# Order of the products of a quad: all bfloat16 products together, the float32 products with the edge weights behind them

## The reference

```
parts = [x[src], x[dst]] (+ [e of the layer before], from the second layer on)
e     = relu(concat(parts) @ We + be)
agg   = segment_sum(e * norm[:, None], dst)
x     = relu(concat([x, agg]) @ Wn + bn)
```

## Time and profile before

| | |
|---|---|
| Median of three runs | 2226.51 us |
| The three runs | 2226.42, 2226.51, 2234.25 us |
| Span of the profiled execution | 2225.8 us |
| Mean granted TensorE clock | 0.926 of 2.4 GHz |
| PE, DVE, POOL busy, share of the span | 87%, 65%, 47% |

### The profile page before, as it was taken

The page is one execution under the profiler, slowest core; times in us unless marked ns, Lnnn a source line. Parts: engine busy times, 40 slices in busy tenths (PEclk is TensorE's granted clock), DMA queues, the critical chain, the costliest instruction groups (busy, mean ns, idle before and its releaser), DMA issues. The chain is left out here.

```text
span 2225.8 us, 48362 instructions
## 1 busy us (share of the span) xinstructions
PE 1936.7 (87%) x14264; PEld 1459.2 (66%) x14264; DVE 1438.0 (65%) x4661; ACT 648.2 (29%) x1271; POOL 1042.2 (47%) x1015
## 2 busy tenths in 40 slices
PE   6777769999999997488888885999999969999995
PEld 3322225444454544378888865999999859999993
DVE  6999962223231412678898864777777658787885
ACT  0156871212121211233333332333333322111111
POOL 0588850000000000177777734666666347777770
PEclk8687879999999998699999997999999989999998
DMA  3023682000000000645555534777777445555551
GB/s 98 12 60 86 105 103 3 1 0 0 0 0 0 0 0 27 226 147 148 154 154 155 148 101 127 217 218 215 216 214 216 139 115 155 144 155 148 154 148 41
DMA packets 193650, 242.15 MB, mean 109 GB/s; under 512 B 56276, under 2 KB 120047, under 8 KB 192799
## 3 DMA queue, kind: packets, MB, share of 16 engines
q1 hardware_dynamic: 161023, 172.73, 27.7%
q0 software_dynamic: 31840, 57.21, 11.3%
q10 hardware_dynamic: 576, 9.44, 1.1%
HBM read 149.75 MB, written 69.88 MB: 99 GB/s over the span
## 5 line engine op out<-in xcount | busy, mean ns | idle before, releaser
L1514 POOL DMA_INDIRECT rows<-p_dram,src_i x864 | 827.4, 958 | 349.3 <-issue 239.3
L1746 DVE TENSOR_TENSOR agg_t<-psum,agg_t 128x128 f32 x1380 | 390.7, 283 | 192.1 <-PE psum L1625 170.6
L1605 PE MATMUL psum<-w_c,before 128*128 128x128 f32 x1840 | 411.1, 305 | 0.0
L893 PE MATMUL psum<-adj,parts 128*128 (+2 forms) x1750 | 339.8, 351 | 5.3 <-ACT agg L972 4.4
L1594 PE MATMUL psum<-p_sb,pair_src 128*128 x1032 | 230.4, 307 | 108.5 <-DVE pair_dst L1720 66.9
L1679 ACT ACTIVATE rows<-rows 128x512 f32<-128x512 f32 x216 | 136.1, 630 | 575.8 <-DVE rows L1739 575.8
L1730 DVE TENSOR_SCALAR hot_w<-col_f,dst_loc,weight 128x128 f32<-128x128 f32 x864 | 301.2, 353 | 0.5
L1605 PEld LDWEIGHTS psum<-w_c,before 128*128 128x128 f32 x1840 | 283.2, 194 | 0.0
L1266 POOL MEMSET agg_t<- 128x3200 f32 x1 | 2.8, 2764 | 589.9 <-POOLq L1029 589.9
L893 PEld LDWEIGHTS psum<-adj,parts 128*128 128x128 f16 x1750 | 153.0, 98 | 190.9 <-issue 23.6
L1601 PE MATMUL psum<-q_parts,hot_all 128*128 x2592 | 252.2, 220 | 0.0
(11 more groups left out here) (241 smaller groups left out, 2486.1 us busy)
## 6 DMA issues: line engine op xcount, KB each, us to landing
e_dram<-after SPq DMA_DIRECT2D x230, 256.0 KB
before<-e_dram SPq DMA_DIRECT2D x230, 256.0 KB
adj<-stage SPq DMA_DIRECT2D x196, 97.8 KB
pair_rows<-sorted_rows SPq DMA_DIRECT2D x129, 128.0 KB
rows<-p_dram,src_i POOLq DMA_INDIRECT x864
hot_all<-dst_rows ACTq DMA_DIRECT2D x2, 3072.0 KB, 14.7
p_dram<-p_sb SPq DMA_DIRECT2D x6, 384.0 KB
records<-record_of,place_i POOLq DMA_INDIRECT x128
```

Source lines behind the costliest of these rows:

```text
L893: mm = nc.tensor.matmul(psum[:, AGG_BANK, 0:n_cols], parts[:, w, part, :], adj[:, w, cols], start=(w == 0 and part == 0), stop=(w == WINDO ...
L1514: nc.gpsimd.indirect_dma_start(out=rows[:, b % ROWS, m * D:(m + 1) * D], out_offset=None, in_=p_dram, in_offset=bass.IndirectOffsetOnAxis( ...
L1605: mm = nc.tensor.matmul(o, before[:, q % BEFORE, m * P:(m + 1) * P], w_c[:], start=False, stop=True)
L1746: nc.vector.tensor_tensor(a, psum[:, A_BANKS[q % len(A_BANKS)], m * P:(m + 1) * P], a, ALU.add).then_inc(agg_on, 1)
```

## The change

In `products`, a quad's work is issued by kind in place of by tile: first (sorted quads) the four float32 products of line 1594, then the twelve bfloat16 products, then (second and third pass) the four float32 products with `w_c`. The number of instructions of each kind, their operands, the waits ahead of them and the release behind the last one stay. `start=True` now stands on the first product of the quad alone, and `skip_group_check=True` is new on these products. In a rest quad of the first pass, which has bfloat16 products alone, the order stays.

```diff
--- before.py
+++ after.py
@@ -1588,22 +1588,28 @@
                     pe.wait_ge(hot_t_on, b + 1)
                 if e_before is not None:
                     pe.wait_ge(before_in[q % BEFORE], 16 * (q // BEFORE + 1))
+                def sums(m):
+                    return psum[:, E_BANKS[q % len(E_BANKS)], m * D:(m + 1) * D]
+
+                if i is not None:
+                    for m in range(QUAD):
+                        nc.tensor.matmul(sums(m), pair_src[:, i % PAIRS, m, :],
+                                         t["p_sb"][:, bass.ds(values[m], 1), :],
+                                         start=(m == 0), stop=False, skip_group_check=True)
                 for m in range(QUAD):
-                    o = psum[:, E_BANKS[q % len(E_BANKS)], m * D:(m + 1) * D]
                     if i is not None:
-                        nc.tensor.matmul(o, pair_src[:, i % PAIRS, m, :], t["p_sb"][:, bass.ds(values[m], 1), :],
-                                         start=True, stop=False)
                         hot, window = pair_dst[:, i % PAIRS, m, :], values[QUAD + m]
                     else:
                         s = (b * QUAD + m) * P
                         hot, window = hot_all[:, s:s + P], values[(b % 2 + 2) * QUAD + m]
                     for part in range(3):
-                        mm = nc.tensor.matmul(o, hot, t["q_parts"][:, bass.ds(window, 1), part, :],
-                                              start=(part == 0 and i is None),
-                                              stop=(part == 2 and e_before is None))
-                    if e_before is not None:
-                        mm = nc.tensor.matmul(o, before[:, q % BEFORE, m * P:(m + 1) * P], w_c[:],
-                                              start=False, stop=True)
+                        mm = nc.tensor.matmul(sums(m), hot, t["q_parts"][:, bass.ds(window, 1), part, :],
+                                              start=(i is None and m == 0 and part == 0),
+                                              stop=(part == 2 and e_before is None), skip_group_check=True)
+                if e_before is not None:
+                    for m in range(QUAD):
+                        mm = nc.tensor.matmul(sums(m), before[:, q % BEFORE, m * P:(m + 1) * P], w_c[:],
+                                              start=False, stop=True, skip_group_check=True)
                 mm.then_inc(spread, 1)
 
             def turn_and_sum(q):
```

## The result

| | before | after |
|---|---|---|
| Median, us (range, runs) | 2228.99 (2226.42 to 2238.82, 5) | 2213.54 (2211.35 to 2220.12, 5) |
| Span of the profiled execution, us | 2225.8 | 2210.0 |

After / before is 0.9925, with a 95% interval of 0.9906 to 0.9945: the change saves 15.5 us between the medians and 15.8 us between the two profiled spans. Forecast were 2210.0 us and 16.5 us.

What follows compares the result with a forecast made beforehand. PE's own stream was taken to bound the second pass, POOL's gathers the first and third. 15.7 + 0.2 + 0.6 = 16.5 us off the 2225.8 span gives 2209.3, with 0.7 for the median 2210.0 us; range 2203 to 2221.

Steps and rivals of the forecast that it cites:

- The sum: All three passes: 0.2 us saved in the first, 15.7 in the second and 0.6 in the third, together 16.5 us.
- The price of a change of kind: PE's weight loads: each bfloat16 run pays 0.0555 us once, so a quad with three runs fewer saves 0.167 us.
- rival (c): PE's stream: the change of kind isn't what costs 0.0555 us, or the chip sees the order otherwise; 2226 us, chance 0.08.
- The queue behind sorted quads: Second pass: list load of 1.27 us delays addresses, sorted quads 0.11 us late, so 34 of them save only 0.06 each.
- Rival (a): Second pass: list load stays at 1.44 us, 34 sorted quads lose 3.7 us; 2215.7, up to 2218 us, chance 0.17.
- rival (b): Sorted quads don't starve and the third pass's POOL waits shrink with PE's work; 2204 to 2207 us, chance 0.15.
- The Trainium skill's 64 instructions for TensorE's queue: PE's queue: not counted on; with it every sorted quad would keep its 0.167 us, the sum 3.7 us lower.
- The run of twelve in rest quads: Rest quads: first address leads by 1.7 us where 0.9 would do, so all 0.167 us are kept.
- Rival (d): Rest quads: the run of twelve is paced by its addresses, 0.43 us more each; 2256 us with sorted ones, chance 0.06.
- the 81 ns per matmul at 128 columns: PE's load and matmul pairs: by this pace a rest quad takes 1.89 us, the time about 2239 us; chance 0.02.
- The start of the second pass: First four quads, partly at a granted clock of 0.50: change of kind at twice its price, 0.8 us saved.
- The third pass: 0.8 us at the start and 0.5 at the end, less lower-clock work: 0.6 off, ends 3 gained and 3 lost.

Runs made afterwards that it cites:

- e5: Changed kernel with each quad issued in two halves of two tiles, each ordered by kind, giving two runs of six bfloat16 products; 2220.16 us.
- e3: Kernel before, in its old order, with only the flags changed: the start flag on a quad's first product alone; 2227.59 us.
- e2: Kernel before with the new order in sorted quads alone, rest quads in the old order; 2231.31 us.
- e6: Changed kernel with a sorted quad's list load issued earlier, between the transposes and sums ahead of it, in the first and second pass; 2212.86 us.
- e10: Kernel before with fourteen float32 products of constants ahead of sorted quads that follow a sorted quad, in the first and third pass; 2228.97 us.
- e4: Changed kernel with the new order kept in the second pass alone, first and third pass as in the kernel before; 2212.64 us.
- e1: Kernel before with the new order in rest quads alone, sorted quads in the old order; 2219.71 us.
- e7: Changed kernel with SP's store in the second pass issued one quad later, behind the load of `before`; 2212.07 us.
- e8: Changed kernel with fourteen float32 products of constants ahead of sorted quads that follow a sorted quad, in the first and third pass; 2206.35 us.

## Why the prediction was right, step by step

**The sum.** Between the spans 15.8 us went: 0.6 in the first pass, 17.9 in the second (14.8 of them from the fifth quad on) and -2.8 in the third, with 0.1 outside. Forecast were 0.2, 15.7 (14.9 from the fifth quad on) and 0.6. The total is closer than its parts: the start of the second pass gave 2.3 us more than forecast and the third pass 3.4 less, and that the two nearly cancel is luck. The median is 3.5 us above the forecast: 0.7 in the span, 1.4 in an offset (I put a run's time 0.7 us above its span, but in every run with both numbers it lies 1.9 to 2.3 above; the profiled run of the kernel after took 2212.09 us for 2210.0), and 1.4 by which that run lies below the median.

**The price of a change of kind** was 0.0555 us a run, by two run lengths of two stages. e5 and the change measure 0.0535, and 0.160 per rest quad in place of 0.167: 11.2 us for 11.7. That it is the order which costs it, e3 shows; rival (c) is out.

**The queue behind sorted quads** was the unknown, and its account held: a list load of 1.27 us was taken, 1.24 measured, started 1.88 us ahead by forecast and 1.87 by the trace, with the store moved to its start. The sorted quads gave 3.1 us for the 3.2 forecast, which is in part luck too, since they did not give it where I put it: the 27 ordinary ones 27 x 0.121 = 3.3, the seven further ones 0.8, and the seven behind these lost 1.0, since there the store goes out 0.8 us ahead of a list load of 1.4 to 1.75 us. Rival (a) is what e2 has, rival (b) what e6 has in the second pass. 11.2 + 3.1 leave 0.5 of the 14.8 us; 0.3 of it is the difference between the rest quads' median and their mean (3.114 us before, 2.947 after). The Trainium skill's 64 instructions for TensorE's queue ("TensorE: Matmul & The Clock Gate", specification table) don't show here: with room for them no sorted quad could be late by the prediction's account, and the list load again starts with 17 loads and their matmuls to go. By the trace 16 loads have yet to start at each of the 41 list loads of the second pass from its sixth quad on, before and after alike, while the time to the quad goes from 1.77 to 1.87 us.

**The run of twelve in rest quads** wasn't paced by its addresses: 0.73 us in 1504.41 to 1505.14. Rival (d) is out. So is, for this kernel, the 81 ns per matmul at 128 columns of the same page's section "Back-to-back issue gap": it is 60 ns here.

**The start of the second pass**, 0.8 forecast, measured 3.1 (29.1 to 26.0 us for the first four quads). This size isn't settled. The three kernels with the old order in that pass (before, e3, e10) have 27.6 to 29.1 us there, the six with the new one 26.0 to 27.8: the means are 1.6 apart, and the ranges overlap. The pair compared here shows more than most would.

**The third pass** is the step that failed, in its sign: "mostly POOL covers that, not at the end. I take 0.6 off". It lost 2.8 us, just inside its ends. The sum had 0.8 us for the pass's start and 0.5 for its last quads, so it left 0.7 for work at the lower clock. The 0.8 did not come through: POOL's run is 378.6 us before and after. What lies behind POOL's last gather goes from 6.8 to 9.6 us. The last sorted quad, which I had named as the uncovered place, accounts for it: at the lower clock it is 4.24 - 2.77 = 1.47 us longer, and it starts 2.77 us ahead of the end of POOL's last gather (2158.0) in place of 4.27 (2176.52), 1.5 later. The work behind it gives 0.2 back.

This end is no accident of one trace. PE idles 0.5 to 0.8 us ahead of the last sorted quad in the three kernels with the old order and no added products there (before, e3, e4), and 3.4 to 4.2 us in the six with a new order, whole or in part (after, e1, e2, e5, e6, e7). From slot 111 on the first three take 15.2 to 15.5 us, the six 19.7 to 21.1. That the low clock is the cause of the longer quad, e8 shows.

So I had the mechanism and priced it too low. Part of the price was to be had: PE gets ready earlier by what it saves, the gather does not come earlier, so the idle time grows just where nothing lies on top. The rest was not: PE idles 3.55 us longer there, and 1.8 of it is the gather: behind its end on POOL, DVE's addition starts after 3.56 us, in place of 1.75. Why it lands so late (DVE waits 3.51 us for it, 0.45 before) is not settled; no run here tells it apart.

## What to carry to other kernels

Where PE is the bound, count the changes of kind in its stream, since each run of bfloat16 loads between float32 ones pays once more (0.0535 us here); then check that whatever feeds the long run (addresses, list loads) can lead it by the time that the old alternation gave it for free. A saving on an engine that waits elsewhere is not neutral: it turns into idle time, and the next work can start at a lower clock (six of seven such quads of the third pass after, three before), which costs where nothing covers it. Filling such gaps with products of constants paid where they were longer than the filling (e8), and not where most of them were shorter (e10).

## What the runs showed of the hardware

A list load of sixteen window numbers takes longer beside a store from SBUF, and how much longer depends on where the store is issued. With none near it, in the third pass, it takes 1.10 us. With the store behind its start it takes 1.10 to 1.11 us when the store comes 0.7 us behind (e6) and 1.10 to 1.29 when it comes 0.1 behind (after). With the store ahead it takes 1.41 to 1.57 us at 0.4 us ahead (before), 1.39 to 1.75 at 0.6 to 0.8 (after, behind a further quad), 1.21 to 1.37 at 1.2 (before, behind a further quad), and at 1.7 mostly 1.10 to 1.28 again (e7, with five of 27 at 1.42 to 1.61). Stores and list loads are in different queues, and I had expected no such link before reading.

Each address instruction is 46 ns long, but sixteen need 2.0 us of PE's queue, in e2 (1522.1 to 1524.1) as before.
